# A batch's first product moved ahead of the previous batch's second product

## What is computed

```python
y = einsum('bsi,boi->bso', x, weight[adapter_ids])         # first product
logits = y @ gate_w.T + expert_bias                        # 4 experts
one_hot = jax.nn.one_hot(argmax(logits), 4)
base = einsum('bth,oh->bto', y, W_up)                      # second product
z = einsum('nh,erh->ner', y, lora_A)                       # rank 8
delta = einsum('neh,ne->nh', einsum('ner,ehr->neh', z, lora_B), one_hot)
out = x + base + delta
```

## Time and profile before

| | us |
|---|---|
| median of 3 runs (lowest, highest) | 399.13 (398.69, 399.27) |
| profiled execution, first to last instruction | 397.9 |
| TensorE busy | 379.4 (95%) |
| VectorE busy | 213.9 (54%) |
| ScalarE busy | 145.4 (37%) |
| GpSimd busy | 17.5 (4%) |

### The profile page before, as it was taken

How to read it: one execution, slowest core, us unless ns; L and a number is a source line. 1 busy time by engine, 2 the same in 40 slices (tenths; PEclk the granted TensorE clock), 3 DMA queues, 4 the chain that set the end, 5 groups by cost and what they waited for, 6 DMA issues and landing times.

```text
span 397.9 us, 6753 instructions
## 1 busy us (share of the span) xinstructions
PE 379.4 (95%) x2240; PEld 355.0 (89%) x2240; DVE 213.9 (54%) x484; ACT 145.4 (37%) x316; POOL 17.5 (4%) x17
## 2 busy tenths in 40 slices
PE   2899869999999999999999999999999999999996
PEld 2689759889998999889998899988999899988996
DVE  3768495645546347456366455473573553654132
ACT  4766620637015340356105470153503452053100
POOL 0007520000000000000000000000000000000000
PEclk9999988999999999999999999999999999999999
DMA  6897856652096322971257611864229712450002
GB/s 187 300 360 224 261 216 190 239 203 82 24 285 202 146 105 84 273 230 45 105 137 283 213 50 55 248 225 160 105 60 267 234 71 105 146 170 0 0 0 105
DMA packets 21365, 63.65 MB, mean 160 GB/s; under 512 B 2544, under 2 KB 3696, under 8 KB 21360
## 3 DMA queue, kind: packets, MB, share of 16 engines
q1 hardware_dynamic: 21072, 63.07, 47.8%
q10 hardware_dynamic: 288, 0.52, 0.4%
HBM read 55.20 MB, written 8.39 MB: 160 GB/s over the span
## 4 chain that ended last, share of the span: by engine, by line
PE 87%; DMA 4%; DVE 4%; ACT 2%; SPq 1%; issue 1%; POOL 1%; ACTq 0%
PE ps_o L461 31%; PE ps_y L450 28%; PE ps_y L452 14%; PE ps_o L470 13%; PE ps_o L485 2%; DMA w_raw<-w_dram 2%; DMA lb_raw<-lora_b_dram 2%; DVE w_lo L346 2%; DVE x_hilo L339 1%; ACT up_hi L280 1%; POOL up_lo L244 1%; PE ps_y L478 0%; SPq L133 0%; SPq L149 0%; SPq L197 0%
## 5 line engine op out<-in xcount | busy, mean ns | idle before, releaser
L450 PE MATMUL ps_y<-x_hilo,w_hi 128*128 128x512 f32 x512 | 180.3, 397 | 9.4 <-DVE w_lo L346 7.8
L452 PE MATMUL ps_y<-x_hilo,w_lo 128*128 128x256 f32 x512 | 142.7, 279 | 0.0
L450 PEld LDWEIGHTS ps_y<-x_hilo,w_hi 128*128 128x128 f32 x512 | 96.8, 189 | 32.7 <-issue 7.4
L452 PEld LDWEIGHTS ps_y<-x_hilo,w_lo 128*128 128x128 f32 x512 | 97.0, 189 | 0.0
L346 DVE TENSOR_TENSOR w_lo<-w_raw,w_hi 128x512 fp32r<-128x512 f32 x128 | 81.4, 686 | 3.5 <-ACT w_hi L276 1.3
L461 PE MATMUL ps_o<-up_hi,y_hi 128*128 128x366 f32 x256 | 75.9, 337 | 1.9 <-POOL up_lo L244 1.9
L461 PE MATMUL ps_o<-up_lo,y_hi 128*128 128x366 f32 x256 | 74.8, 333 | 0.0
L461 PE MATMUL ps_o<-up_hi,y_lo 128*128 128x366 f32 x256 | 74.8, 333 | 0.0
L276 ACT CAST w_hi<-w_raw 128x512 fp32r<-128x512 f32 x128 | 71.3, 621 | 2.3 <-DMA w_raw<-w_dram 2.1
L296 ACT COPY y_small<-ps_y 128x256 f32<-128x256 f32 x64 | 23.8, 372 | 121.4 <-PE ps_y L452 121.4
L396 DVE TENSOR_TENSOR y_full<-ps_y,y_small 128x256 f32<-128x256 f32 x64 | 27.1, 424 | 68.8 <-ACT y_small L296 68.8
(11 more groups left out here) (33 smaller groups left out, 177.8 us busy)
## 6 DMA issues: line engine op xcount, KB each, us to landing
w_raw<-w_dram SPq DMA_DIRECT2D x63, 512.0 KB, 4.1
rows<-x_dram SPq DMA_DIRECT2D x16, 512.0 KB, 5.3
x_raw<-xT_dram SPq DMA_DIRECT2D x30, 256.0 KB, 7.0
up_raw<-w_up_dram SPq DMA_DIRECT2D x8, 512.0 KB, 6.7
out_dram<-rows SPq DMA_DIRECT2D x8, 512.0 KB, 7.7
out_dram<-rows SPq DMA_DIRECT2D x8, 329.0 KB, 7.2
out_dram<-rows SPq DMA_DIRECT2D x8, 183.0 KB, 6.7
x_raw<-xT_dram ACTq DMA_DIRECT2D x2, 256.0 KB, 3.4
```

What stands on the lines that cost most here:

```text
L450: pe.matmul(ps_y[c % 2][:, :], w_hi[:, c % RING, cols], x_hilo[:, k, :], start=(k == 0), stop=False)
L452: last = pe.matmul(ps_y[c % 2][:, S:2 * S], w_lo[:, c % RING, cols], x_hilo[:, k, 0:S], start=False, stop=(k == KC - 1))
```

## The change

TensorE does the first products of batches 0 and 1, then the second product of batch 0, the first product of batch 2, the second product of batch 1, and so on; at the end the second products of batches 6 and 7 follow each other. y_hi and y_lo have two buffers. ScalarE's and VectorE's lists follow the same order: the first product's part of batch b + 1 (with the splitting of x and w of batch b + 2 behind it) stands ahead of the second product's part of batch b. Ahead of the first product of batch 1 now stands, on both engines, only the splitting of x and w tiles 0 to 3 of that batch. The splitting of w_up is spread: up_hi of tile 0 behind tile 6 of batch 0, of tile 1 behind tile 7, of tiles 2 to 7 behind tiles 1 to 6 of batch 1; `gate_hi` moves to tile 0 of batch 1 and lora_b behind the product of batch 1. SyncE loads batch 1's x and w tiles 0 to 3 ahead of w_up, then w tile c and w_up tile c in turn for c of 4 to 7. TensorE gets waits on out_ready, since y_ready no longer implies that the PSUM banks of the second product have been read. All loops are written out. GpSimd's list stays as it is.

```diff
-    UP_AFTER = {4: (0, 1), 5: (2, 3), 6: (4, 5), 7: (6, 7)}
+    UP_AFTER = {(0, 6): (0,), (0, 7): (1,), (1, 1): (2,), (1, 2): (3,), (1, 3): (4,), (1, 4): (5,), (1, 5): (6,),
+                (1, 6): (7,)}
...
-        y_hi = sb("y_hi", [P, OC, S], F32R)
-        y_lo = sb("y_lo", [P, OC, S], F32R)
+        y_hi = sb("y_hi", [P, 2, OC, S], F32R)
+        y_lo = sb("y_lo", [P, 2, OC, S], F32R)
...
+            i = adapter(1)
+            for q in range(XQ):
+                load_x(1, q)
+            for c in range(RING):
+                load_w(1, c, i)
             sp.dma_start(gl_raw[:, :, :], gl[:, :, :]).then_inc(gl_in, 16)
             for c in range(RING):
                 load_up(c)
-            for q in range(XQ):
-                load_x(1, q)
             for c in range(RING, OC):
+                load_w(1, c, i)
                 load_up(c)
...
-                    if first:
-                        if c == min(UP_AFTER):
-                            gate_hi()
-                        for u in UP_AFTER.get(c, ()):
-                            up_hi_part(u)
-                if first:
+                    if (b, c) == (1, 0):
+                        gate_hi()
+                    for u in UP_AFTER.get((b, c), ()):
+                        up_hi_part(u)
+                if b == 1:
                     lora_b_hi()
...
-            batch(0, first=True)
-            with act.Fori(1, B - 1) as b:
-                batch(b)
-            batch(B - 1, last=True)
+            first_product(0)
+            for b in range(B):
+                if b + 1 < B:
+                    first_product(b + 1)
+                second_product(b)
...
-                if not last:
+                if b + 2 < B:
                     for c in range(RING // 2, RING):
-                        w_lo_part(b + 1, c)
+                        w_lo_part(b + 2, c)
...
+            first_product(0)
+            for c in range(RING // 2, RING):
+                w_lo_part(1, c)
+            for b in range(B):
+                if b + 1 < B:
+                    first_product(b + 1)
+                second_product(b)
...
-            with nc.Fori(0, B, engines=(mybir.EngineType.PE,), hint_back_edge=True) as b:
-                first_product(b)
+            first_product(0)
+            for b in range(B):
+                if b + 1 < B:
+                    first_product(b + 1)
                 pe.wait_ge(gl_ready, 1)
+                if b > 0:
+                    pe.wait_ge(out_ready, b * 6 - 3)
```

More of the change, by code:

```diff
@@ L290, in lora_b_hi, with first_product @@
                 act.copy(eye[:, :], eye_f[:, :]).then_inc(eye_ready, 1)
-            def batch(b, first=False, last=False):
+            def first_product(b):
                 for c in range(OC):
@@ L312, in batch, with second_product @@
                         w_hi_part(b + 1, c)
+            def second_product(b):
                 for t in range(T):
@@ L389, in finish, with first_product @@
                                       rows[:, t, part], ALU.add).then_inc(out_ready, 1)
-            def batch(b, first=False, last=False):
+            def first_product(b):
                 for c in range(OC):
                     dve.wait_ge(y_small_ready, b * OC + c + 1)
-                    if c >= 2 or not first:
+                    if c >= 2 or b > 0:
                         dve.wait_ge(y_hi_ready, b * OC + c - 1)
@@ L400, in batch @@
                     dve.wait_ge(y_hi_ready, b * OC + c + 1)
-                    dve.tensor_tensor(y_lo[:, c, :], y_full[:, c % 2, :], y_hi[:, c, :].bitcast(F32),
+                    dve.tensor_tensor(y_lo[:, b % 2, c, :], y_full[:, c % 2, :], y_hi[:, b % 2, c, :].bitcast(F32),
                                       ALU.subtract).then_inc(y_ready, 1)
-                    if first:
-                        for u in UP_AFTER.get(c, ()):
-                            if u % 2 == 0:
-                                up_lo_part(u)
-                if not last:
+                    for u in UP_AFTER.get((b, c), ()):
+                        if u % 2 == 0:
+                            up_lo_part(u)
+                if b + 1 < B:
                     for q in range(XQ):
@@ L411, in batch, with second_product @@
                         w_lo_part(b + 1, c)
-                if first:
+            def second_product(b):
+                if b == 0:
                     dve.wait_ge(bias_in, 16)
@@ L429, in _ @@
                 w_lo_part(0, c)
-            batch(0, first=True)
-            with dve.Fori(1, B - 1) as b:
-                batch(b)
-            batch(B - 1, last=True)
+            first_product(0)
+            for c in range(RING // 2, RING):
+                w_lo_part(1, c)
+            for b in range(B):
+                if b + 1 < B:
+                    first_product(b + 1)
+                second_product(b)
         @block.tensor
@@ L469, in bank_c @@
                 for y, up, end in terms if c < OC - 1 else terms[::-1]:
-                    last = pe.matmul(ps_o[t][:, 2, 0:end - 2 * CUT], y[:, c, toks], up[:, c, 2 * CUT:end],
+                    last = pe.matmul(ps_o[t][:, 2, 0:end - 2 * CUT], y[:, b % 2, c, toks], up[:, c, 2 * CUT:end],
                                      start=(c == 0 and end == NW), stop=(c == OC - 1 and end == NW))
@@ L494, in _ @@
                     pe.wait_ge(y_ready, b * OC + c + 1)
-                    bank_ab(0, c)
-                    bank_c(0, c)
+                    bank_ab(b, 0, c)
+                    bank_c(b, 0, c)
+                if b > 0:
+                    pe.wait_ge(out_ready, b * 6 - 2)
                 for c in range(OC):
-                    bank_c(1, c)
+                    bank_c(b, 1, c)
                 pe.wait_ge(eye_ready, 1)
+                if b > 0:
+                    pe.wait_ge(out_ready, b * 6 - 1)
                 for c in range(OC):
@@ L512, in _ @@
                 add_lora(1, 1)
+                if b > 0:
+                    pe.wait_ge(out_ready, b * 6)
                 for c in range(OC):
-                    bank_ab(1, c, (0,))
+                    bank_ab(b, 1, c, (0,))
                 add_lora(1, 0)
```

53 lines of the change are left out of this document (24 added, 29 removed).

## The result

| | before | changed |
|---|---|---|
| median of the runs on one chip (4 each) | 398.91 us | 407.18 us |
| profiled execution, first to last instruction | 397.9 us | 404.3 us |
| TensorE busy | 379.4 us (95%) | 379.4 us (94%) |

The ratio is 1.0213, with a 95% interval of 1.0178 to 1.0249. The change makes the kernel slower, by 6.4 us between the two profiled executions and by 8.3 us between the medians. The forecast was 404.7 us, within 400.5 to 409 us; for the profiled execution it was 403.5 us.

What follows compares the result with a forecast made beforehand. TensorE's own work was taken to bound the kernel from 67.35 us on, with 8.42 us lost before. 6.6 + 2.3 + 5.1 - 8.4 = +5.6 us made the span 403.5 us and the median 404.7 us, range 400.5 to 409 us.

Steps and rivals of the forecast that it cites:

- What is removed: Between batch 0's first product and the next one: TensorE's lost 8.42 us (two stalls and slow clock) all go.
- The hole: Between the first products of batches 0 and 1: TensorE idle because x_hilo has one buffer, 6.6 us.
- the hand-over of 5.26 us: From a second product's start through y_small, x_hi, x_lo and w_lo to TensorE's next start; 5.26 us of The hole.
- The slow clock: Start of batch 1's first product: TensorE at half clock after its idle time, some 8 matmul pairs slowed, 2.3 us.
- The waits inside: Batch 1's first product: TensorE stalls at tiles 4, 5 and 6, 0.9 + 2.2 + 2.0 = 5.1 us, between 0 and 7.4.
- At nothing: Rest of the kernel: out_ready waits met, last second product unchanged, no matmul, copy or byte added, loop edges give nothing.
- rival (c): Batch 0's second product: the z chain's stall comes back; if missed by as much as before, 411 us; chance 0.07.
- (d): All engines: written-out lists make an engine wait for its instructions; no row prices it, nearest 3.8 us; chance 0.04.
- (e): TensorE's seven loop edges give time back, at most 0.22 us each, 1.5 us: 403.2 us; chance 0.02.
- (a): Batch 1's first product runs without stalls: +0.5 us, 399.6 us; chance 0.08.
- (b): Faster: idle time, slow clock and inner stalls together stay below 8.4 us; -1.8 us, 397.3 us; chance 0.07.
- The 1.2 us added to the span: From profiled span to median: 399.13 us stood 1.2 us above the span, so 403.5 us became 404.7 us.

Runs made afterwards that it cites:

- e12: Changed kernel with w_up tiles 0 and 1 loaded ahead of batch 1's adapter number, x and w; 404.61 us, ratio 1.0129.
- e8: Changed kernel with 60 extra unread matmuls of 256 columns in the idle time between the first products of batches 0 and 1; 405.94 us, ratio 1.0185.
- e9: As e8, with 72 instead of 60 unread matmuls; 406.79 us, ratio 1.0210 to the kernel before.
- e2: As e1, with w_up tiles 0 and 1 split behind tile 0 of batch 1 instead of tiles 6 and 7 of batch 0; 401.24 us, ratio 1.0070.
- e6: As e2, with all low parts of w_up and lora_b on VectorE, GpSimd keeping only the gate columns; 400.18 us, ratio 1.0052.
- e1: Changed kernel with w tiles 4 to 7 of batch 1 issued on SyncE ahead of w_up tiles 4 to 7; 403.88 us, ratio 1.0133.
- e3: Changed kernel with gate_hi behind tile 5 of batch 0 instead of tile 0 of batch 1; 405.86 us, ratio 1.0186.
- e4: Kernel before, with the loops of SyncE, ScalarE, VectorE and TensorE written out and nothing else; 398.49 us, ratio 1.0007.
- e5: As e1, with batch 1's x split during batch 0's product into room of up_lo tiles 4 to 7, splitting of w and w_up moved accordingly; 396.57 us, ratio 0.9954.
- e7: As e5, with all low parts of w_up and lora_b on VectorE; 397.11 us, ratio 0.9975.
- e10: As e7, with w_up's parts behind later tiles, w tile 3 split in batch 1, lora_b's low halves between the z chains; 395.17 us, ratio 0.9917.
- e11: As e10, with lora_b's high half one tile earlier and its low halves behind tiles 6 and 7 of batch 1; 394.60 us, ratio 0.9901.

## Why the prediction was right, and where its terms were off

**What is removed: right.** The whole 8.42 us of the earlier trace rows are gone; the second product takes 24.51 us.

**The hole: right in kind, 2.07 us too small.** Forecast 6.6, measured 8.67 us. The step that failed is the landing of w_up tile 0, put at 33.2 us and in truth at 35.4 us. Three of its inputs were wrong. Ahead of its issue the bytes did not flow at the 426 GB/s of the earlier trace rows but at 158 and 268 GB/s in the stages shown (201 GB/s from 20.96 to 26.88 us). Behind its issue they did flow at 408 GB/s, but w_up tiles 1 to 3, which the sum left out, shared the engines: some 4.7 MB instead of 3.8. And w tile 3 of batch 1 is not issued when SyncE comes to it: four issues take 2.68 us there and 2.08 us in e12, for the ring of w has to be freed by w_lo of batch 0's tile 7. The wider bound, 7.9 us, came from one tile's bytes; it was still short. e12 shows that this landing is all of the error: without it the hole is 6.27 us, a little under the forecast. In e8 and e9, where F0 ended earlier, the same landing made it 9.30 and 9.08 us. The rest of the working, the hand-over of 5.26 us from the earlier trace rows, stands beside 5.17 us in e2.

**The slow clock: 2.3 forecast, 1.5 us measured.** The mechanism is right. What it costs is the part of the slow stretch that is left when TensorE starts again. In the changed kernel the clock is low for 6.8 us, 3.8 us of them in the hole; in e12, with the same 6.8 us and a shorter hole, it costs 2.5 us, and in e2 3.1 us. So the two errors, +2.07 and -0.8 us, are partly one. But the length of the hole does not settle it: e6 has the 5.01 us of e2 and pays 2.2 us, and e1, idle for 8.22 us, pays 2.2 us too. What sets the start and the length of the slow stretch stays open. The price of 0.64 us for a pair holds. Two readings beside it in the prediction do not: the earlier trace rows show one dip and none in the first slice, and where the earlier trace rows were read the profile gives a granted clock of 1.00.

**The waits inside: 5.1 forecast, 4.9 us measured** from tile to tile, against tiles of 2.78 us (56.17 for 55.69 us; 61.44 for 58.95; 66.13 for 64.22: 0.5 + 2.5 + 1.9). The idle times read 0.31, 2.22 and 1.65 us; the other 0.7 us are the matmul pipeline's end and restart. The forecast had 0.9 + 2.2 + 2.0. Their sum fits better than the first of them, 0.5 for 0.9. The path through gate columns, GpSimd's up_lo, the raw ring, SyncE and w tile 6 is shown by e1 and e3, the lock by e6; w tile 6 was put at 52.7 us on the queue and 57.0 us landed, and was there at 53.71 and 58.2 us, 1 us late in a product that started 2.1 us late.

**The sum.** Measured: 8.67 + 1.5 + 4.9 - 8.4 = +6.7 us at the end of the second product, +6.4 us in the span; forecast +5.6. The terms agree better than they had a right to, since they aren't additive: e9 takes the clock's 1.5 us away and gets nothing, and e12 wins 2.6 us at the start and 2.0 at the end. That they came so near in sum is in part luck.

**At nothing: right.** No wait on out_ready shows, the z chain of batch 0 is in time (rival (c) did not come), and writing out the loops moves nothing (rivals (d) and (e), e4). Rivals (a) and (b) did not come: even e6, nearly free of inner waits, stays 0.5% above before.

**From profile to median.** The medians differ by 8.3 us, the profiles by 6.4; against the forecast of 5.6 us the profiles miss by 0.8 us and the medians by 2.7 us. The 1.2 us added to the span was wrong for both kernels. Of the kernel before, the profiled span of 397.9 us was on the long side: in the experiments' comparisons its median spans are 396.4 to 397.0 us. Of the changed one 404.3 us is the shortest of four (up to 405.3). And what lies outside the span is 2.1 us where before it is 1.8. What sets that 0.3 us stays open: e4, e5 and e12 have about 2.1 us as well, e7, e10 and e11, written out too, 1.8.

## What to carry to other kernels

A reordering that removes a stall also removes the cover of everything that the moved work used to hide; look for the single buffer that the two now neighbouring stages share, and give it a second place first (e5, e11), or the stall only changes its name. Work that is done once, such as splitting a weight, should be placed by the room of each engine in each tile, and each of its loads counts in the queue that it shares with the loads of the path. Do not add the prices of a hole, the slow clock behind it and later waits: each absorbs part of the one before.
